# Cross-attention kernel: context rows loaded in two pieces one slot earlier, and the output leaving PSUM by another engine

## The reference

```python
a = layer_norm(ctx) * gamma + beta            # over the 512 features
Q, K, V = x @ Wq.T, a @ Wk.T, a @ Wv.T        # split into 16 heads of 32
attn = softmax(Q K^T / sqrt(32))              # mask: all ones here, still applied
out = x + tanh(gate) * (concat(attn V) @ Wo.T)
```

## Time and profile before

| | |
|---|---|
| median of 3 runs | 1159.52 us (1155.87 to 1161.36) |
| the profiled execution | 1151.25 us, span 1149.4 us |
| mean granted TensorE clock in it | 0.953 |
| main stage (PE), from the product of slot 0 to that of slot 126 | 113.9 to 1111.3 us |

### The profile page before, as it was taken

The page is one execution under the profiler, slowest core; times in us unless marked ns, Lnnn a source line. Parts: engine busy times, 40 slices in busy tenths (PEclk is TensorE's granted clock), DMA queues, the critical chain, the costliest instruction groups (busy, mean ns, idle before and its releaser), DMA issues.

```text
span 1149.4 us, 31949 instructions
## 1 busy us (share of the span) xinstructions
PE 1025.9 (89%) x11665; PEld 852.0 (74%) x11665; DVE 774.2 (67%) x1446; ACT 645.2 (56%) x1332; POOL 680.7 (59%) x945
## 2 busy tenths in 40 slices
PE   8796989989989989899898889898889898999995
PEld 7795877778777767687777767777777677878873
DVE  4640477776676677667666777666767866787775
ACT  2312565665565656565556656655556566666662
POOL 1346866666666756567557556676566556776211
PEclk9898999999999999999999999999999999999997
DMA  9443222222232332223323322232233222322111
GB/s 274 158 148 71 98 78 75 88 72 86 86 97 87 97 95 82 66 75 89 95 86 97 94 80 78 66 96 87 87 96 95 84 78 68 94 76 73 33 33 40
DMA packets 82772, 102.26 MB, mean 89 GB/s; under 512 B 28544, under 2 KB 65408, under 8 KB 82720
## 3 DMA queue, kind: packets, MB, share of 16 engines
q10 hardware_dynamic: 24232, 56.60, 15.1%
q1 hardware_dynamic: 58488, 44.94, 14.5%
HBM read 91.34 MB, written 10.19 MB: 88 GB/s over the span
## 4 chain that ended last, share of the span: by engine, by line
DMA 65%; DVE 16%; PE 12%; issue 4%; POOL 2%; SPq 1%; ACT 0%; DVEq 0%; ACTq 0%; POOLq 0%
DMA row_max<-rmax 34%; DMA x<-row_max 25%; PE bank L765 9%; DVE rmax L708 4%; DVE shared_f L718 3%; DVE stats L651 3%; DMA rows<-in_ctx 3%; DMA row_stats<-row_stat 3%; DVE bank L698 2%; PE sbank L859 1%; DVE top L695 1%; PE bank L875 1%; DVE mv L656 1%; DMA shared_f<-in_xT 1%; POOL cn L408 0%
## 5 line engine op out<-in xcount | busy, mean ns | idle before, releaser
L765 PE MATMUL bank<-w_v,shared_r 128*125 128x512 f32 x1152 | 312.5, 424 | 77.0 <-DVE xy L689 77.0
L765 PEld LDWEIGHTS bank<-w_v,shared_r 128*125 128x125 f32 x1152 | 229.6, 202 | 135.9 <-issue 84.2
L708 DVE TRANSPOSE_TENSOR_REDUCE rmax<-shared_f 128x14 f32<-128x448 f32 x384 | 216.3, 614 | 158.5 <-DMA row_max<-rmax 131.1
L765 PE MATMUL bank<-shared_r,w_k 128*128 128x376 f32 x1536 | 300.7, 345 | 10.1 <-ACT shared_f L606 9.5
L765 PEld LDWEIGHTS bank<-shared_r,w_k 128*128 128x128 f32 x1536 | 260.8, 190 | 32.2 <-issue 20.9
L584 ACT ACTIVATE shared_f<-shared_f 125x448 f32<-125x448 f32 x384 | 204.3, 580 | 133.9 <-DVE shared_f L718 133.8
L438 POOL TENSOR_TENSOR shared_f<-shared_f 125x448 f32<-125x448 f32 x128 | 151.0, 1179 | 177.9 <-ACT shared_f L584 164.7
L553 ACT ACTIVATE shared_f<-sbank,mask_b 125x448 f32<-125x448 f32 x384 | 215.6, 635 | 69.2 <-PE sbank L859 69.1
L718 DVE TENSOR_TENSOR shared_f<-shared_f,bank 125x448 f32<-125x448 f32 x384 | 215.5, 617 | 4.5
L613 ACT ACTIVATE shared_f<-bank 125x512 f32<-125x512 f32 x96 | 57.3, 597 | 160.2 <-PE bank L765 160.1
L695 DVE TENSOR_REDUCE top<-x 128x14 f32<-128x168 f32 x128 | 56.0, 437 | 120.9 <-DMA x<-row_max 120.9
(11 more groups left out here) (64 smaller groups left out, 950.6 us busy)
## 6 DMA issues: line engine op xcount, KB each, us to landing
cn<-in_ctxT ACTq DMA_DIRECT2D x30, 750.0 KB, 6.2
rows<-in_ctx ACTq DMA_DIRECT2D x28, 750.0 KB
stat_bc<-row_stats ACTq DMA_DIRECT2D x29, 375.0 KB, 4.2
x<-row_max SPq DMA_DIRECT2D x128, 84.0 KB
xy<-in_x SPq DMA_DIRECT2D x32, 224.0 KB, 3.1
out<-xy SPq DMA_DIRECT2D x32, 224.0 KB, 4.9
shared_f<-in_xT SPq DMA_DIRECT2D x7, 896.0 KB, 8.4
rows<-in_ctx SPq DMA_DIRECT2D x4, 750.0 KB
```

Source lines behind the costliest of these rows:

```text
L708: last = dve.tensor_reduce(rmax[:, BLK * j:BLK * j + BLK], prob[:, (r - 1) % NB, j, :].rearrange("p (k a) -> p k a", a=32), AX.X, ALU.max, ...
L765: last = pe.matmul(dst, l, m, start=(start and k == 0), stop=(stop and k == len(pairs) - 1))
```

## The change

Five things are changed.

1. The load of `rows` is made of two DMAs, of partitions 0 to 119 and of 120 to 124. Both add to `ld_rows`, whose target per batch becomes 32.
2. ACT issues them in the slot `u == 2` instead of `u == 3`, still behind the wait for `stats_done` and ahead of the copy of K.
3. DVE does all of a batch's row statistics in `u == 1` (`statistics`), where it did a third there and the rest in `u == 2`.
4. The output leaves its bank by ACT, in `u == 2`, multiplied by the gate, into a new buffer `gated`; this sets a new semaphore `y_out`, for which PE waits in the place of `y_done`.
5. GpSimd adds `gated` to `xy` at the end of its slot `u == 3` and sets `y_done`, on which SP's store of the result waits.

```diff
         def load_rows(queue, i, c):
             if behind(i, 2, c):
                 wait_apart(queue, stats_done, i * 2 + c)
-            queue.dma_start(rows[0:SP_, :, :], rows_v[i * 2 + c, :, :, :]).then_inc(ld_rows, 16)
+            for part in (slice(0, 120), slice(120, SP_)):
+                queue.dma_start(rows[part, :, :], rows_v[i * 2 + c, part, :, :]).then_inc(ld_rows, 16)
...
+            def result(i, c):            # GpSimd
+                if c % 2:
+                    wait_apart(pool, ld_x[1], (i + (c + 1) // 2) * 16)
+                else:
+                    wait_apart(pool, ld_x[0], (i + c // 2 + 1) * 16)
+                wait_apart(pool, y_out, i * 2 + (c + 1))
+                pool.tensor_tensor(xy[0:T, c % 2, :], xy[0:T, c % 2, :], gated[0:T, :], ALU.add) \
+                    .then_inc(y_done, 1)
...
                 if live(i, LOOP, r - 3, SLOTS):
                     sum_chunks(i, r)
+                if u == 3 and live(i, 2, c - 2, B):
+                    result(i, c - 2)
...
-                    if live(i, 2, c + 5, B) and behind(i, 2, c + 2):      # ACT, under u == 3
-                        load_rows(act, i, c + 5)
+                if u == 2 and live(i, 2, c + 5, B) and behind(i, 2, c + 2):
+                    load_rows(act, i, c + 5)
...
+                if u == 2 and live(i, 2, c - 2, B):                       # ACT, end of its slot
+                    b = c - 2
+                    act.wait_ge(y_mm, i * 2 + (b + 1))
+                    if behind(i, 2, b):
+                        act.wait_ge(y_done, i * 2 + b)
+                    act.activation(gated[0:T, :], bank[VO[0]][0:T, :], ACT.Copy, scale=gat[0:T, 0:1]) \
+                        .then_inc(y_out, 1)
...
-                dve.scalar_tensor_tensor(xy[0:T, c % 2, :], bank[VO[0]][0:T, :], gat[0:T, 0:1],
-                                         xy[0:T, c % 2, :], ALU.mult, ALU.add).then_inc(y_done, 1)
...
                 if u == 1 and live(i, 2, c + 4, B) and behind(i, 2, c + 2):     # DVE
-                    bn_rows(i, c + 4, (0,))
-                if u == 2 and live(i, 2, c + 4, B) and behind(i, 2, c + 2):
-                    bn_rows(i, c + 4, (1, 2))
-                    bn_join(i, c + 4)
-                if u == 2 and live(i, 2, c - 2, B):
-                    result(i, c - 2)
+                    statistics(i, c + 4)
...
                 if r % KT == 3 and live(i, 2, c - 3, B):                        # PE, project_v
-                    pe.wait_ge(y_done, i * 2 + (c - 2))
+                    pe.wait_ge(y_out, i * 2 + (c - 2))
```

More of the change, by code:

```diff
@@ L109, in xattn @@
         xy = sb("xy", [128, 2, D])
+        gated = sb("gated", [128, D])
         ident = sb("ident", [128, 128])
@@ L198, in xattn @@
         y_mm = sem("y_mm")
+        y_out = sem("y_out")
         y_done = sem("y_done")
@@ L641, in x_group, with statistics @@
                       xr_hi, i * 2 + g, xr_done)
[L643 to L650, removed]
+            def statistics(i, c):
+                dve.wait_ge(ld_rows, i * 64 + (c + 1) * 32)
+                if not first_two(i, c):
+                    dve.wait_ge(row_stat_done, i * 2 + (c - 1))
+                if isinstance(i, int) and 2 * i + c > 0:
+                    dve.wait_ge(stats_done, 2 * i + c)
+                for j in range(ST):
                     dve.bn_stats(stats[0:SP_, j, :], rows[0:SP_, j, :]).then_inc(bn_step, 1)
-            def bn_join(i, c):
                 wait_apart(dve, bn_step, i * (2 * ST) + (c + 1) * ST)
@@ L657, in bn_join @@
                 last.then_inc(stats_done, 1)
-            def statistics(i, c):
-                bn_rows(i, c, range(ST))
-                bn_join(i, c)
             def weight_lo(n, raw, dst):
@@ L843, in output @@
                 else:
-                    pe.wait_ge(y_done, i * 2 + c)
+                    pe.wait_ge(y_out, i * 2 + c)
                 product(bank[VO[0]][0:T, :],
```

## The result

The changed kernel takes 1084.85 us (median of 4 runs, 1082.81 to 1089.74); the kernel before takes 1157.69 us beside it. The ratio is 0.938 (95% interval 0.933 to 0.942). The forecast was 1026 us with a range of 1006 to 1075, so the direction was right and the size wrong: 1085 is where rival 1 stood, which had 12%.

The account below looks back on a forecast made before the run. The exchange of maxima through HBM was taken as the bound, with PE next at 28.0 us per batch. 1151.25 - 116 (steady slots) - 14 (start) + 1 (end) = 1022, plus 4 for the median: 1026 us, range 1006 to 1075.

Parts of the forecast that it names:

- rival 1: Exchange of maxima stays the bound at 30.0 us per batch, above PE's 28.0: 1067 to 1106 us, middle 1085; chance 12%.
- The start: Before PE's slot 0: a wider row load shortens the wait for batch 3's rows, -14 us (8 to 20).
- The end: Last batch: ACT 0.6 and POOL 1.35 us replace DVE's one instruction, +1 us (between nothing and 2).
- The transfer: ACT's load of rows as 120 and 5 partitions: spread over more engines it takes 2.4 us, against 6.1 on five.
- The two collisions: Rows meet the exchange of u=2, up to 2.4 us; `cn` and `stat_bc` meet that of u=3, 3.1 us.
- the exchange's spare time: An undisturbed exchange repeats in 5.65 us, 1.35 less than PE's slot, so lateness of at most 4.2 us is worked off.
- the tail: Past the last row load, a store 2.1 us late was back on time while PE kept 7.00 us per slot.
- PE's wait for L689 goes: 77.0 us idle, and with it the low clock: ACT empties the output's bank, so PE's slots take 7.00 us: gain 119.4 over 119 slots, of which -116 is counted.
- The offset: Median of runs over the profiled execution: 8.3 us before, of which +4 was added to the forecast.
- The unchanged cost of ACT's hold: ACT's wait for the statistics, 49.8 us in 28, moves to u=2, where they are finished before ACT comes.
- Rival 2: ACT, held in u=2 for the statistics, delays the copy of K: +42 us, 1190 us; chance 3%.
- rival 3: The row load stays as long but L689's way is free: 1125 to 1155 us, say 1145; chance 5%.

Follow-up runs that it names:

- one_dma_u2: The changed kernel with the rows in one DMA of 125 partitions again, still issued in u=2: 1133.8 us, ratio 0.986 to the kernel before.
- apart_125: The changed kernel with rows loaded as three DMAs of 125 partitions, one third each in u=2, u=3 and u=0: ratio 0.975 to the kernel before.
- exit_only: The kernel before with only the result path changed (ACT empties the bank with the gate, GpSimd adds): 1150.0 us, ratio 1.001.
- load_only: The changed kernel with its result path undone (DVE takes the output out, PE waits for y_done): 1077.9 us, ratio 0.937 to the kernel before.
- few_rows: The changed kernel with steady row loads cut to 10 of 125 partitions, ACT's wait kept: 1016.2 us, ratio 0.884 to the kernel before.
- thirds: The changed kernel with the 120 partitions loaded in three DMAs of 2 KB per partition, all in u=2: 1077.4 us, ratio 0.940 to the kernel before.

## Why the prediction was wrong

- **The bound and the reason for the slow store: right.** The exchange held the chain, five engines carried the rows, and the way out was to shorten what its store meets. The split spreads the load (window above).
- **The start: right in size.** -14 was predicted; -12.9 to slot 0, by the split alone (one_dma_u2 and apart_125 stay at 113.9 and 112.1).
- **The end: right.** +1 predicted (0 to 2), +1.6 measured.
- **The transfer: undersized.** "I take 2.4" us for the rows on 15 engines. From the page's share of ACT's queue (below) it is 3.5 if it is 15 engines, an estimate, and in the windows it lasts about 5 us, in part beside the load of `x`. The two collisions together cost about 5.0 (3.1 on the store by the rows, 1.9 on the load of u=2 by `cn` and `stat_bc`), against 5.5 in the prediction, so this alone would not have broken it.
- **The step that failed** is the exchange's spare time, "1.35 less than PE's slot", and with it "lateness is at most 2.4 - 1.35 + 3.1 = 4.2 us and is worked off over the next slots". 1.35 us per slot were not there. In u=3 DVE's stretch with the normalising takes 6.9 us, in u=1 the exchange takes 6.9 too, with the store of a finished batch on one side and DVE's statistics, as long, on the other; only u=0 with 5.8 is free. Added up as the chain runs, undisturbed exchange 5.65 + 6.9 + 5.8 + 6.9 is 25.2, with 5.0 of collisions 30.2, and that is what the trace shows. The chain's whole spare time per batch is 2.8 us, and 5.0 had to fit. The prediction had this sum in rival 1 (30.0) and set it aside for the tail, where the store was 2.1 us late once and recovered; but with only one collision per batch, of 3.1 us, and without the statistics. A recovery from a single late event says nothing about a lateness that comes in each batch. The other support, that PE had waited for nothing but L689 while the chain was 7.3 us late, was worse: PE could only wait at the first thing that came late, and exit_only shows the wait move to the next.
- **"PE's wait for L689 goes: 77.0 us idle, and with it the low clock"**: the wait went, the time did not. Of the predicted -116 in the steady part 53 came, and parts 4 and 5 had no share in it (load_only, with parts 1 to 3, has it too).
- **The offset: too large.** +4 was added for the median over the profiled execution; the median of after is 0.3 us below it.
- **The unchanged cost of ACT's hold: right.** few_rows keeps it and is bound by PE.
- **Rival 1** was what happened, at its middle (1085); its 12% came from trust in the tail. That it met the number so well is in part luck: its sum of 30.0 had the stages at 24.5 where they are 25.2, and the collisions at 5.5 where they are 5.0, with the second on the wrong transfer. The stated range did not take in "most of rival 1" either: it ended at 1075, and rival 1 went from 1067 to 1106. Rival 2's mechanism did not show; rival 3 fell, since the load does spread.

The Trainium skill's rule on two transfers to disjoint partition halves (DMA: Bandwidth & Descriptors, rules for kernel authors: use one transfer) doesn't hold for 125 partitions: its reason is that each half already runs on all 16 engines, and here the single transfer keeps 0.31 of them busy. one_dma_u2 and the changed kernel differ in nothing else, and have 0.986 and 0.938. What the same page says on the number of engines (the section on why a DMA increments its semaphore by 16) agrees with the window of before, 0.31 for 5 of 16; the 0.80 to 0.88 of the window after show that it is many more than five, not that it is 15.

## What to carry to other kernels

Where a chain of waits is cyclic (each slot's exchange waits for the one before), add up its stages over one period, each with what it meets, and compare the sum with the next bound; spare time in one undisturbed stage must not be multiplied by the number of stages. A wait of the busiest engine names what came late first, not what has to be made faster: removing it alone (exit_only) moved 77 us by one instruction. A small transfer in a chain of waits shares its engines with bulk loads, so it paid here to make these wide (0.986 to 0.938), cut them in pieces and give each piece a stage that has time for it (0.896).

## What was not expected of the hardware

**The same load on more engines takes more engine time.** One engine's time added to another's is meant, as the profile counts it. The rows of the page for the DMA queues (ACT's is q10), of the kernel after, of one_dma_u2 and of few_rows:

```profile
q10 hardware_dynamic: 24652, 56.60, 20.0%
```

```profile
q10 hardware_dynamic: 24232, 56.60, 16.1%
```

```profile
q10 hardware_dynamic: 21152, 36.82, 12.3%
```

Shares times 16 engines times the span (1082.9, 1131.6, 1014.5 us) are 3465, 2915 and 1997 us. The difference to few_rows, over 28 loads, is 52.4 us of engine time for a load of 120 + 5 partitions and 32.8 for one of 125; few_rows still loads 60 of the 750 KB. So 690 KB go at 13.5 GB/s per busy engine when spread and at 21.5 on five. Over 15 engines 52.4 us would be about 3.5 us a load and not 2.2. By the same sum the kernel before gives 27.9 us and thirds, with 2 KB per partition, 42.8. The difference takes the other loads' packet times as equal in both kernels, but the windows say the same without it: 172 GB/s at a share of 0.80 (574 to 575, above) is 13.4 GB/s per busy engine, and 126 at 0.31 is 25.4. It isn't a ceiling of all engines together, since with `cn` in flight the windows reach 324 and 378 GB/s. What limits it isn't settled: no run changed the source's layout or the partitions' order.

**Smaller pieces of the rows moved the delay and did not remove it.** With 2 KB per partition and DMA instead of 6 (thirds), store and load of u=2 take 9.9 us in sum instead of 10.4: the store is 0.9 us shorter on average, what follows it 0.8 longer.
